# Routing by an inverted list and gathered rows in experts_0, and a retention layer without a query projection

## What is computed

```python
shared = (silu(x @ sh_gate_w.T) * (x @ sh_up_w.T)) @ sh_down_w.T      # 704 hidden columns
probs = softmax(x @ router_weight.T)                                   # 8 experts
top_v, top_i = top_k(probs, 2); top_v = top_v / top_v.sum(-1, keepdims=True)
for e in range(8):                                                     # 176 hidden columns each
    gate, up = split(x @ gate_up_proj[e].T)
    out += (silu(gate) * up @ down_proj[e].T) * combine[:, e:e + 1]
out += sigmoid(x @ shared_gate_w.T) * shared
```

## Time and profile before

| what | us |
|---|---|
| median of 3 runs | 1033.25 |
| lowest, highest run | 1031.84, 1033.46 |
| profiled execution, its own time | 1036.44 |
| span of that execution, first to last instruction | 1034.9 |
| PE busy (matmuls) | 972.2 |
| DVE, ACT, POOL busy | 714.2, 599.7, 415.3 |
| mean granted clock of TensorE, 1 is full speed (2.4 GHz) | 0.987 |

### The profile page before, as it was taken

The page is one execution under the profiler, slowest core; times in us unless marked ns, Lnnn a source line. Parts: engine busy times, 40 slices in busy tenths (PEclk is TensorE's granted clock), DMA queues, the critical chain, the costliest instruction groups (busy, mean ns, idle before and its releaser), DMA issues. The chain is left out here.

```text
span 1034.9 us, 20928 instructions
## 1 busy us (share of the span) xinstructions
PE 972.2 (94%) x7027; PEld 802.5 (78%) x7029; DVE 714.2 (69%) x2168; ACT 599.7 (58%) x1518; POOL 415.3 (40%) x406
## 2 busy tenths in 40 slices
PE   8899999999998997889996899999999998989988
PEld 6677778777875655778776698988988896778877
DVE  7777777777765478523448577877777786569994
ACT  2177777777784773322132777777777875334433
POOL 5767676767654102241342543434344441010000
PEclk9999999999999999989998999999999999999999
DMA  5360222022003300462330310101101100001111
GB/s 180 72 203 12 63 53 63 12 63 42 2 1 108 121 2 1 153 184 67 98 112 22 127 33 27 39 17 30 36 15 41 26 11 1 0 1 47 47 34 54
DMA packets 28248, 57.39 MB, mean 55 GB/s; under 512 B 4678, under 2 KB 15686, under 8 KB 26406
## 3 DMA queue, kind: packets, MB, share of 16 engines
q1 hardware_dynamic: 26294, 51.20, 17.2%
q0 software_dynamic: 1872, 5.13, 1.4%
HBM read 41.75 MB, written 9.21 MB: 49 GB/s over the span
## 5 line engine op out<-in xcount | busy, mean ns | idle before, releaser
L527 ACT ACTIVATE sb_a_P<-sb_a_nS,sb_a_nm 128x257 f32<-128x257 f32 x256 | 127.5, 507 | 86.4 <-DVE sb_a_nm L638 86.2
L437 POOL TENSOR_TENSOR sb_a_P<-sb_a_P,sb_a_rec 128x512 f32<-128x512 f32 x128 | 129.3, 1042 | 87.5 <-DVE sb_a_rec L649 87.1
L638 DVE CUSTOM_DVE_ANT_0 sb_a_nS<-a_pS,sb_a_mask,sb_a_nsink 128x256 f32<-128x256 f32 x256 | 109.3, 478 | 39.4 <-PE a_pS L786 39.4
L2179 ACT ACTIVATE sb_a_t<-a_pp,sb_a_w 64x512 f32<-64x512 f32 x128 | 87.5, 683 | 14.9 <-PE a_pp L146 6.0
L2251 DVE SCALAR_TENSOR_TENSOR sb_a_t<-a_pp,sb_a_w,sb_a_cs 128x512 f32<-128x512 f32 x64 | 47.7, 745 | 57.9 <-ACT sb_a_t L2179 57.9
L2103 POOL TENSOR_TENSOR sb_a_qT<-sb_a_t 128x512 f32<-128x512 f32 x32 | 41.2, 1289 | 109.6 <-DVE sb_a_t L2254 109.6
L146 PE MATMUL a_pp<-sb_x_high,sb_a_w_low 128*128 128x512 f32 x184 | 78.1, 425 | 6.8 <-DVE sb_a_P L593 3.9
L146 PE MATMUL a_pp<-sb_x_high,sb_a_w_high 128*128 128x512 f32 x184 | 72.8, 396 | 0.0
L146 PE MATMUL a_pp<-sb_x_low,sb_a_w_high 128*128 128x512 f32 x184 | 72.4, 393 | 0.0
L536 ACT COPY sb_xn<-a_pT 128x512 f32<-128x512 f32 x128 | 67.9, 583 | 1.9 <-PE a_pT L800 1.9
L800 PE MATMUL a_pT<-sb_ident,sb_a_P 128*128 128x128 f32 x512 | 68.2, 276 | 0.3 <-ACT sb_xn L536 0.3
(11 more groups left out here) (455 smaller groups left out, 2904.2 us busy)
## 6 DMA issues: line engine op xcount, KB each, us to landing
sb_a_kr<-sb_a_kall SPq DMA_DIRECT2D x28, 256.0 KB, 4.1
sb_f_w<-f_w SPq DMA_DIRECT2D x12, 384.0 KB, 4.5
sb_a_w<-a_w SPq DMA_DIRECT2D x16, 257.0 KB, 2.7
m_sorted<-m_blank SPq DMA_DIRECT2D x1, 2967.0 KB, 14.5
sb_m_xg<-m_sorted SPq DMA_DIRECT2D x11, 258.0 KB, 3.1
sb_m_egu<-m_egu SPq DMA_DIRECT2D x2, 1408.0 KB, 8.2
sb_a_w<-a_w SPq DMA_DIRECT2D x8, 259.0 KB, 2.8
sb_a_wo<-a_wo SPq DMA_DIRECT2D x8, 256.0 KB, 2.7
```

Source lines behind the costliest of these rows:

```text
L437: nc.gpsimd.tensor_tensor(part, part, rec[b % 2][:, h, :].rearrange("p (q o) -> p q o", o=1) .to_broadcast([P, 2, S]), ALU.mult).then_inc( ...
L527: out = nc.scalar.activation(Pm[b % 2][:, h, qt, 0:S + 1], nS[:, h, qt, 0:S + 1], ACT.Exp, bias=nm[b % 2][:, h, qt:qt + 1], scale=-1.0, ac ...
L638: out = nc.vector.tensor_tensor_reduce(nS[:, h, qt, 0:S], pS[h][:, qt * S:(qt + 1) * S], wmask[:, qt, :], -1.0, nsink[par][:, h:h + 1], AL ...
L2179: out = nc.scalar.activation(t2[n][a, :, :].rearrange("p b s -> p (b s)"), pp[n][b, :], ACT.Identity, bias=bias[b])
```

## The change

In experts_0:

- xn loses its two extra columns. SP writes it twice to a DRAM tensor x_rows of 2048 rows (four DMAs, two token halves by two copies), and the blank list and its copy in cross_attention_0 are gone.
- DVE makes the first half of `times_up(0)` ahead of the ranking and the second half behind it. PE counts between the two halves of gate_up(0).
- The sorted list is inverted without a scatter. DVE splits pos into slot and place within the slot and writes two sets of 0/1 matrices (in_slot: 16 of 128 x 128, named: 16 of 128 x 46, both bf16). PE multiplies them in 16 matmuls (`invert`), which gives for every place in the list the number of the row that stands there. `numbers()` on DVE turns this into from_row and to_row.
- POOL gathers the rows of each slot from x_rows by an indirect DMA (23 in all, ring of 4 pairs) in place of SP's loads. Its scatter of the products stays, and the two alternate. `name_pair` is gone.
- M0_FRONT is 3 instead of 4: three shared tiles on either side of the pairs.
- The additions of the routed products (`add_products`) move: one half behind shared tile 4's work on DVE, one behind tile 5's.
- The memory of the first two stages is freed before experts_0.

In retention_1: since q k^T = x Wh Wh^T ctx^T, PE forms G = Wh Wh^T from a second copy of the weights (x1_wt, fetched with the others), K' = G ctx^T takes the place of KT, and the scores use xT itself. QT is gone. The order is now G, V, K', the turning of xn, the scores.

The diff, cut to its core:

```diff
-M0_FRONT = 4
+M0_FRONT = 3
-M0_ROW = D + 2
-M0_RING = 3
+M0_RING = 4
...
         @block.sync                                   # cross_attention_0
             k.fetch(sp, src, "a1")
-            sp.dma_start(k.sorted_rows, src["m0_blank"]).then_inc(k.blank_in, 16)
...
+            def rows_to_dram(half):                   # experts_0, SP
+                sp.wait_ge(k.norm_of_m0.xn_ready, (half + 1) * HALF)
+                for c in range(2):
+                    rows = x_rows[c * T + half * NC:c * T + (half + 1) * NC].rearrange("(t p) n -> p t n", p=P)
+                    sp.dma_start(rows, k.xn[:, half * HALF:(half + 1) * HALF, :]).then_inc(x_out, 16)
+
+            rows_to_dram(0)
             gate_up_of(2)
             for d in range(KD):
                 sp.dma_start(egu[d][:, :], src["m0_egu"][d]).then_inc(egu_in, 16)
-            gate_up_of(3)
+            rows_to_dram(1)
             down_of(2)
             for c in range(2):
                 sp.dma_start(edn[c][:, :], src["m0_edn"][c]).then_inc(edn_in, 16)
-            gate_up_of(4)
-            down_of(3)
-            sp.wait_ge(sent, 16 * 2 * NT)
-            for j in range(M0_RING):
-                rows_of(j)
-            gate_up_of(5)
-            down_of(4)
-            down_of(5)
-            for j in range(M0_RING, PAIRS):
-                rows_of(j)
+            for n in range(3, M0_TILES):
+                gate_up_of(n)
+                down_of(n)
...
+            pool.wait_ge(x_out, 16 * 4)               # POOL; gather(j), scatter(j): one indirect DMA per slot
+            pool.wait_ge(numbered, 2)
+            for j in range(M0_RING):
+                gather(j)
+            pool.wait_ge(numbered, 5)
+            for j in range(PAIRS):
+                scatter(j)
+                if j + M0_RING < PAIRS:
+                    gather(j + M0_RING)
...
+            times_up(0, (0,))                         # DVE; then the ranking as before, up to pos
+            times_up(0, (1,))
+            nc.vector.tensor_scalar(pos_in[:, :], pos[:, :], P - 1, None, ALU.bitwise_and).then_inc(shown, 1)
+            nc.vector.tensor_scalar(pos_tile[:, :], pos[:, :], 0x7fffff80, None, ALU.bitwise_and).then_inc(shown, 1)
+            nc.vector.tensor_tensor(in_tile[:, :, :], ..., ALU.is_equal)      # 128 x 368
+            nc.vector.tensor_tensor(named[:, :, 0:M0_SLOTS], ..., ALU.mult)   # 128 x 368
+            nc.vector.tensor_scalar(named[:, :, M0_SLOTS:2 * M0_SLOTS], in_tile[:, :, :], token, None, ALU.mult)
+            for g in range(4):
+                nc.vector.tensor_tensor(in_slot[:, js, :], ..., ALU.is_equal)  # 128 x 512
...
             for n in range(M0_TILES):                 # DVE
...
-                times_up(n)
-                down_low(n)
-                h_low(n)
+                if n > 0:
+                    times_up(n)
+                h_low(n)
+                if n == 0:
+                    numbers()
+                down_low(n)
+                if n == 0:
+                    owners()
+                    shares()
+                if n >= LAST - 1:
+                    add_products(n - (LAST - 1))
...
+            def invert():                             # PE
+                for j in range(2 * NT):
+                    pe.wait_ge(shown, 6 + j // 4)
+                    out = nc.tensor.matmul(acc[3][:, 0:2 * M0_SLOTS], in_slot[:, j, :], named[:, j, :],
+                                           start=(j == 0), stop=(j == 2 * NT - 1))
+                out.then_inc(inverted, 1)
+
+            gate_up(0, halfway=count)
+            gate_up(1)
+            invert()
+            pe.wait_ge(lg_ready, 1)
+            pe.wait_ge(ranked, 5)
+            for a in range(3):
+                clear(a)
             down(0)                                   # waits for numbers() and clears acc[3] before its last tiles
...
             for h in range(X1_H):                     # retention_1, PE
+                out = nc.tensor.matmul(bb[3][:, h * P:(h + 1) * P], wt[:, h, :], wt[:, h, :], start=True, stop=True)
+            out.then_inc(squared, 1)
...
-                    nc.tensor.matmul(ba[j % 4][:, :], wh[:, h, :], k.xT[:, h, half * NC:(half + 1) * NC],
+                    nc.tensor.matmul(ba[j % 4][:, :], G[:, h, :], cT[:, h, half * NC:(half + 1) * NC],
                                      start=True, stop=True).then_inc(filled, 1)
+            on_tensor(pe)
```

319 lines of the change are left out of this document (162 added, 157 removed).

## The result

Six runs of the changed kernel beside six of the kernel before, on the same chip: 1037.72 us median (1036.41 to 1043.5) against 1033.38 (1031.84 to 1034.22), ratio 1.0052 with a 95% interval of 1.0028 to 1.0076. The change makes the kernel slower by about 5 us. The forecast was 1027.5, in a range that ended at 1031.0. The changed kernel itself was measured again later beside other kernels, with a ratio of 1.0048 (1.0031 to 1.0064); one of its six executions there took 3357.2 us and is left out of it.

What follows compares the result with a forecast made beforehand. TensorE, busy 94% of the span, was taken as the bound, with gaps in experts_0. Terms -2.2 (experts_0's stage), -3.4 (its end) and -3.3 (retention) summed to -8.9, giving 1027.5 us for profile and runs; range 1020.5 to 1031.0.

Steps and rivals of the forecast that it cites:

- Pairs: Pair loop: PE sets the 4.97 us period; POOL's 5.04 us issue per round is absorbed by the second yb buffer, costing nothing.
- Rival (3): Pairs: POOL becomes the bound, each indirect DMA held for one DVE operation; +12.3 us, 1039.8; chance 0.06.
- The wait for tile 3: At turn_pair(0): PE waits 5.1 us (2.3 to 8.0) for hT, held up by gate_up tile 3's later load.
- I take the middle, 12.0 us: Gate_up tile 3's load: time to landing, between 9.2 and 14.9 us, putting the landing at 452.5.
- slow end: Gate_up tile 3's load: 14.9 us to landing, from the row of 1.97 MB in 16 us beside scatters.
- which have 14 us: Pair 0's gathered rows, first gather at about 440: 14 us of room if the x-row writes land late.
- By the same durations: End of experts_0: last additions start 6.2 us after the last gate_up instead of 9.6, -3.4 us.
- The front: Start of experts_0: PE runs through without the 4.80 us gap; down(0) starts 4.2 us earlier than 444.63.
- The clock behind the wait: After PE's wait at turn_pair(0): 2.3 us lost at the lower clock.
- Retention: Before retention's scores: the query projection goes and the xT wait stays, -3.3 us.
- The stall: Experts_0, fifth matmul of down(1) at 457.86: unexplained stop under the last scatters, taken as gone, -5.6 us.
- The choice that the runs hold less of it than the profile: Unexplained stall: the profile's 3.2 us above the median put down to it, so runs hold 2.4 of 5.6.

Runs made afterwards that it cites:

- e2: Changed kernel with gather(j + 4) issued ahead of scatter(j) on POOL: 1033.18 us, ratio 1.0003.
- e3: Changed kernel with POOL's gathers two pairs further ahead, gathers 4 and 5 before the scatter loop: 1032.43 us, ratio 1.0001.
- e1: Changed kernel with gate_up tile 3's load issued on SP ahead of down_of(2) and the edn loads: 1033.26 us, ratio 0.9997.
- e14: Changed kernel with three yb buffers instead of two, POOL's order unchanged: ratio 1.0068.
- e15: e4 with ACT's casts of attention_1's first weights one shared tile earlier: ratio 0.9935.
- e11: Changed kernel with ACT's casts of attention_1's first weights one shared tile earlier: ratio 1.0057.
- e6: e5 with ACT's casts of attention_1's first weights one shared tile earlier and y's loads ahead of down_of(5): ratio 0.9924.
- e8: Kernel before with counting between gate_up(0)'s halves, hT's first half ahead of the ranking, other clears ahead of down(0): 1032.75 us, ratio 0.9965.
- e9: Kernel before with both edn loads issued on SP behind gate_up tile 3, at 423 instead of 437.85: ratio 1.0014.
- e17: Kernel before with POOL waiting for the end of gate_up(2) between the eighth and ninth scatter: ratio 1.0064.
- e7: Kernel before with the retention part of the change alone: 1033.8 us, ratio 0.9978.
- e5: e4 with both edn loads issued on SP ahead of down_of(2): 1026.56 us, ratio 0.9912.
- e10: e6 with gathers only exchanged with scatters, not two pairs ahead: ratio 0.995.
- e4: Changed kernel with gate_up tile 3's load early on SP and POOL's gathers two pairs further ahead: 1027.44 us, ratio 0.9945.
- e16: e5 with ACT's casts of attention_1's first weights earlier and three yb buffers: 1022.34 us, ratio 0.989.
- e12: Changed kernel with all 16 additions of the routed products again behind down(5): ratio 1.0098.

## Why the prediction was wrong, step by step

The forecast's sum was -8.9 in the profile; the two profiled executions differ by +2.9. The 11.8 us between are these.

**Pairs, +6.0 (forecast 0).** The step that failed is "0.07 over the period in eight pairs, 0.6 us, which the second yb buffer absorbs: nothing". It counted POOL's load and not its order. gather(4) stands behind scatter(0) and so behind y_ready(0): its two operations are issued at 477.53 and 478.83, the rows land 2.8 us after issue (the median of the trace), at 481.6, and turn_pair(4) is due 2.4 us after the first product of pair 3 (478.66), at 481.0. From there every slip returns with the gather four pairs on. e2 and e3, beside e1 on one chip, show that the order is the whole cost, e14 that the buffer named is beside the point. Rival (3) had the right place and the wrong mechanism: the indirect DMAs took 0.96 to 1.00 us beside busy DVE, and no lock held them.

**The wait for tile 3, 8.65 (forecast 5.1, bounds 2.3 to 8.0).** The mechanism was right and the size was off. "I take the middle, 12.0 us" counts from the issue of down_of(2) to the landing of tile 3; measured from 439.77 to 455.3 it is 15.5 us, past even the slow end of 14.9. The slow end was the better row, since the eight gathers, 1.05 MB, were issued from 439.79 on, in the same microseconds as the loads. With its even turns between queues the Trainium skill ("DMA: Bandwidth & Descriptors", section "Queues, rings and completion order") gave an estimate of 14.5 us; by that rule the trace comes out 1.0 us later, but nearer than by the middle. The other traces with this order, with waits of 7.28 to 8.33 us, say the same. And "which have 14 us" for pair 0's rows held only because the load was late: with the load early, the same gathers cost 3.06 us (e1).

**End of experts_0, -2.1 (forecast -3.4).** The additions moved as described. The step that failed is "By the same durations": four took 4.85 us beside POOL. Undoing that conflict gives 1.2 us back (e15, e11, e6). The forecast's own rows give 3.2 and not 3.4 for eight additions of 0.4 us. Another +0.9 stands between DVE's last aggregate and its first operation of attention_1, 3.98 us idle in the changed kernel and 3.97 or 3.98 in every kernel made from it, 3.10 or 3.11 in every one made from the kernel before. Nothing in the forecast spoke of it, and its cause was not found:

```profile
563.32 0.38 DVE L196 BATCH_NORM_AGGREGATE sb_mv<-sb_stats 128x2 f32<-128x6 f32 x4
567.68 1.38 DVE L2278 TENSOR_SCALAR sb_xn<-sb_x,sb_mv,sb_a_root 128x256 f32<-128x256 f32 x4 [3.98 <-PEq L1375]
```

**Right in kind and nearly in size.** The front: down(0) 5.3 us earlier against the same start (forecast 4.2; the inversion took 0.58 us where 1.9 was taken between bounds of nothing and 1.9). The clock behind the wait: 1.9 (2.3). Retention: -3.1 (-3.3), in the traces of the change and alone. The stall: gone, -5.2 (-5.6), and e8, e9 and e17 bear out that it goes with the scatters. The choice that the runs hold less of it than the profile fits the measurement: the profiles differ by 2.9 us, the runs by about 5. It fits e17 too, whose trace is 1.6 us longer than that of the kernel before and whose runs are 6.6 us longer by the ratio. It is not shown by this: the changed kernel's profile, without a stall, lies 1.6 us above its median as well (1039.35 against 1037.72), and on another chip e7's, stall included, lies only 0.4 us above. The rest, the start, attention_1 and the time around the span, is +1.1 in all.

The chances failed with the largest step: slower stood at 0.06 because only a lock on POOL was thought able to reach it. The order on POOL's queue gives 6 us without one.

## What to carry to other kernels

When a queue issues both what feeds a loop and what drains it, put the feeding part ahead of the draining wait; count the latency around the whole loop, not the issue time per round. When a wait is removed by issuing a load earlier, ask which transfer is next in line at the same moment: here the load, the gather behind it and edn were three links of one chain, and each move alone uncovered the next wait. Before an addition of VectorE is moved "under" other work, look at what POOL does with SBUF in that stretch.

## What was not expected of the hardware

- An unbroken train of 16 indirect DMAs on POOL stops PE, ACT and DVE near its end, at a cost of 6 us (some 8 in e8), with no wait in the program: PE's matmuls start 0.7 us or more apart where 0.12 is usual, ACT's next operation is marked "remote". With one pause of 8.16 us in the train no stop shows, up to the last scatter. Moving 1.44 MB of other loads away does not help. What the engines lack in that time was not found.
- Smaller stops of the same look came in the pairs of e5, e6 and e10 (pairs 59.6, 62.3 and 66.5 us, chips 12 and 6) and not in e3, e4, e15 and e16 (55.6 us each, chips 13 and 3). Open.
- Four additions of VectorE beside four subtractions of POOL took 4.85 us instead of 1.66, and a subtraction 1.48 instead of 1.29.
- The pair loop of the change took 60.8 to 61.6 us in four traces (the changed kernel twice, e1, e14) and 67.4 in both of chip 6 (e11, e12).
